# Head 0's queries straight from the projection, and in attentions 3 and 4 the division and half of the maximum's placing on GpSimd

## The reference

```python
def cross(x, ctx, mask, g):              # one layer; LN is a layer norm
    q = heads(LN(x) @ wq + bq); k = heads(ctx @ wk + bk); v = heads(ctx @ wv + bv)
    p = softmax(q @ k.T / sqrt(16) + masked)   # attentions 1, 2: an int mask; 3, 4: none
    if layer == 1: p = p * g                   # attention 1: weights 256 x 4096 after the softmax
    return x + merge(p @ v) @ wo + bo
x = cross_1(x); x += taylor_attention(LN(x)); x += top1_experts(LN(x))
x = cross_2(x); x += frame_attention(LN(x)); x += chosen_experts(LN(x))
x = cross_3(x); x += plain_attention(LN(x)); x += zone_experts(LN(x))
x = cross_4(x); x += recurrence(LN(x));      x += feed_forward(LN(x))
```

## Time and profile before

| | us |
|---|---|
| median of 3 runs | 1430.35 (1428.22 to 1432.22) |
| profiled execution | 1436.41 |
| its span, first to last instruction | 1435.2 |
| busy: TensorE, VectorE, ScalarE, GpSimd | 1263.0, 1016.8, 849.1, 481.5 |
| mean granted TensorE clock | 0.935 of full speed |

### The profile page before, as it was taken

The page is one execution under the profiler, slowest core; times in us unless marked ns, Lnnn a source line. Parts: engine busy times, 40 slices in busy tenths (PEclk is TensorE's granted clock), DMA queues, the critical chain, the costliest instruction groups (busy, mean ns, idle before and its releaser), DMA issues. The chain is left out here.

```text
span 1435.2 us, 29641 instructions
## 1 busy us (share of the span) xinstructions
PE 1263.0 (88%) x10855; PEld 637.1 (44%) x10930; DVE 1016.8 (71%) x2349; ACT 849.1 (59%) x1331; POOL 481.5 (34%) x678
## 2 busy tenths in 40 slices
PE   7899978999998786899999888599998895999987
PEld 6456642333332454233333544244444581444445
DVE  4758789999997245788885243599993336999932
ACT  4632239999997230588888351178886202788852
POOL 1431317889989303344444230211110001111100
PEclk9999987999999878699999999789999996999999
DMA  8699960111140111021132426122243201122300
GB/s 293 193 323 300 331 212 19 45 50 38 39 141 2 45 30 50 19 56 48 46 94 81 151 46 234 50 57 56 68 150 109 74 0 43 56 68 63 116 1 8
DMA packets 115174, 136.61 MB, mean 95 GB/s; under 512 B 13579, under 2 KB 96179, under 8 KB 112956
## 3 DMA queue, kind: packets, MB, share of 16 engines
q1 hardware_dynamic: 107142, 126.55, 28.7%
q10 hardware_dynamic: 7888, 8.16, 1.8%
HBM read 99.73 MB, written 34.90 MB: 94 GB/s over the span
## 5 line engine op out<-in xcount | busy, mean ns | idle before, releaser
L1280 ACT ACTIVATE prob_a<-ps 128x1024 f32<-128x1024 f32 x480 | 468.4, 1019 | 96.8 <-PE ps L1103 57.8
L1085 PE MATMUL ps<-kop,qop 52*128 52x512 f16 x1024 | 302.4, 418 | 58.5 <-DMA qop<-qparts 20.9
L1304 DVE TENSOR_REDUCE best_a<-ps 128x1 f32<-128x512 f32 (+1 forms) x488 | 318.0, 710 | 24.8 <-PE ps L1085 22.8
L1103 PE MATMUL ps<-qop,kop 52*128 52x256 f16 x2048 | 217.1, 279 | 6.2 <-ACT prob_a L1280 2.7
L1132 PE MATMUL ps<-prob_a,vop_a 128*32 128x256 f32 x3072 | 212.8, 398 | 4.7 <-issue 4.7
L1300 DVE CUSTOM_DVE_ANT_0 dump_a<-ps,neg_q 128x512 bf16<-128x512 f32 (+1 forms) x244 | 165.8, 715 | 42.7 <-PE ps L1085 41.5
L1085 PEld LDWEIGHTS ps<-kop,qop 52*128 52x128 f16 x1024 | 73.1, 95 | 241.2 <-DVE best_a L1304 96.7
L1418 POOL TENSOR_TENSOR used_a<-prob_a,gT 128x1024 f32<-128x1024 f32 x64 | 154.0, 2407 | 22.2 <-DVE used_a L1317 19.4
L1396 POOL TENSOR_SCALAR mrest_a<-nmax_a 128x2 f32<-128x2 f32 x64 | 27.8, 434 | 333.1 <-DVE nmax_a L1309 333.1
L1103 PEld LDWEIGHTS ps<-qop,kop 52*128 52x128 f16 x2048 | 92.0, 96 | 105.0 <-issue 52.5
L1132 PEld LDWEIGHTS ps<-prob_a,vop_a 128*32 128x32 f32 x3072 | 86.8, 112 | 89.8 <-issue 57.0
(11 more groups left out here) (382 smaller groups left out, 1752.1 us busy)
## 6 DMA issues: line engine op xcount, KB each, us to landing
kop<-kparts SPq DMA_DIRECT2D x384, 64.0 KB, 2.3
vals<-vst SPq DMA_DIRECT2D x16, 1024.0 KB, 5.7
kparts<-kp SPq DMA_DIRECT2D x64, 256.0 KB, 4.9
vraw<-vals SPq DMA_DIRECT2D x64, 256.0 KB, 3.1
e_w<-in_e_w SPq DMA_DIRECT2D x4, 2048.0 KB, 11.3
z_w<-in_z_w SPq DMA_DIRECT2D x24, 256.0 KB, 6.4
gT<-in_ctxT SPq DMA_DIRECT2D x8, 512.0 KB, 13.3
raw<-in_mask SPq DMA_DIRECT2D x16, 256.0 KB, 3.7
```

Of the source, the lines that this page charges most:

```text
L1085: return pe.matmul(out, qop[rows, h, t * P:(t + 1) * P], kop[rows, h % UNROLL, first:first + CHUNK], start=True, stop=True)
L1103: ins = pe.matmul(st_bank(n)[:, j * NT:(j + 1) * NT], kop[rows, h % UNROLL, at:at + P], qop[rows, h, :], start=(j % 2 == 0), stop=(not add ...
L1280: act.activation(prob[:, n % NP, :], st_bank(n), ACT.Exp, scale=1.0 / SCORE_UNIT).then_inc(S("exp_done"), 1)
L1304: dve.tensor_reduce(out, bank, AX.X, ALU.max).then_inc(sem, 1)
```

## The change

Two parts. In attentions 2 to 4, head 0's queries no longer pass through DRAM: a weight matrix `first_w`, made by GpSimd during the attention before, holds head 0's columns at all their places in `qop`; two matmuls (`project_first`) make high, low and cleared rows at once, and VectorE writes them into `qop` (`set_first`). The loads begin at head 1, and TensorE waits for them and for the cleared rows only at head 1. Constants for this are made by GpSimd in stage 1 (`fill_first`: 15 instructions) from one more small load (`first_b`).

In attentions 3 and 4, ScalarE places the turned maximum in one half, and GpSimd copies it to the other (`copy_max`). The fold's result goes to bank 7 instead of a ring bank, ScalarE reads it out (`read_fold`), and GpSimd divides (`divide`: a power of −1 and a product), for all heads but the last. The order within a head is another, and the C's are 26 ahead instead of 24.

```diff
-PLAIN_ORDER = "CCKKCCV CKCKCCV KCKCF CCTCKKCV CCV".replace(" ", "")
+PLAIN_ORDER = "CCKKCV CKCCKCV CKCCFTKCCKCV CKCCV".replace(" ", "")
...
+    def project_first(self, pe, S, bank):
+        for ct in range(CT):
+            ins = pe.matmul(self.c.ps[:, bank, 0:NT], self.c.first_w[:, ct, :], self.c.xT[:, ct, :],
+                            start=(ct == 0), stop=(ct == CT - 1))
+        ins.then_inc(S("first_q_psum"), 1)
+    def set_first(self, dve, S, bank, high, whole=None, sighted=None):
+        c, l = self.c, self.l
+        found, bias = c.ps[:, bank, 0:NT], c.first_b[:, l:l + 1]
+        dve.wait_ge(S("first_q_psum"), 1)
+        if whole is None:
+            dve.tensor_scalar(high, found, c.low_row[:, 0:1], c.first_b_low[:, l:l + 1], ALU.mult, ALU.add).then_inc(S("first_q_high"), 1)
+            dve.wait_ge(S("first_q_high"), 1)
+            dve.scalar_tensor_tensor(out=c.qop[:, 0, :], in0=found, scalar=bias, in1=high, op0=ALU.add, op1=ALU.subtract)\
+               .then_inc(S("first_q_set"), 1)
+        else:
+            dve.scalar_tensor_tensor(out=whole, in0=found, scalar=bias, in1=sighted, op0=ALU.add, op1=ALU.mult)\
+               .then_inc(S("first_q_whole"), 1)
+            dve.wait_ge(S("first_q_whole"), 1)
+            dve.tensor_scalar(high, whole, c.low_row[:, 0:1], None, ALU.mult).then_inc(S("first_q_high"), 1)
+            dve.wait_ge(S("first_q_high"), 1)
+            dve.tensor_tensor(c.qop[:, 0, :], whole, high, ALU.subtract).then_inc(S("first_q_set"), 1)
...
-        self.c.ops.load_q(eng, self.c.ops.S("q_first"), slice(0, UNROLL), Q_PIECES[half::2])
+        self.c.ops.load_q(eng, self.c.ops.S("q_first"), slice(0 if self.l == 0 else 1, UNROLL), Q_PIECES[half::2])
...
+            sp.dma_start(c.first_b[:, :], c.a["first_b"]).then_inc(S("first_b_loaded"), 16)
...
+            fill_first(c, pool, S)
...
-    banks = (1, 2)
+    banks, first_bank = (2, 7), 4
...
+            q.set_first(dve, S, first_bank, first_high[:, :], first_whole[:, :], sighted[:, :])
             q.clear_blind(dve, S, banks, whole, sighted)
             q.low_of(dve, S, whole)
         else:
+            q.set_first(dve, S, first_bank, first_high[:, :])
...
+        q.project_first(pe, S, first_bank)
+        if l == SHIELDED:
+            pe.wait_ge(S("blind_found"), 1)
         q.project(pe, S, banks)
...
-            sp.dma_start(c.qop[at:at + rows, :, :], c.clear_rows[0:rows, :, :]).then_inc(S("rows_cleared"), 16)
+            sp.dma_start(c.qop[at:at + rows, 1:H, :], c.clear_rows[0:rows, 1:H, :]).then_inc(S("rows_cleared"), 16)
...
-    AHEAD = 32 if weighted else 24
+    AHEAD = 32 if weighted else 24 if by_query else 26
...
-    SUM_AT, TURN_AT = (1, 1) if weighted else (3, 4) if by_query else (3, 5)
+    SUM_AT, TURN_AT = (1, 1) if weighted else (3, 4) if by_query else (3, 4)
...
+    HALVES_SET = HALVES if by_query else 1
+    aside = lambda h: not by_query and h < H - 1
...
+    fold_out = c.ps[:, 7, 0:QT * 32]
...
-            pe.wait_ge(ops.S("q_first" if h < UNROLL else "q_rest"), Q_DONE * (l + 1))
+            if h == 0 and asked is not None:
+                pe.wait_ge(asked.S("first_q_set"), 1)
+            else:
+                pe.wait_ge(ops.S("q_first" if h < UNROLL else "q_rest"), Q_DONE * (l + 1))
...
-                pe.wait_ge(S("max_set"), HALVES * (h + 1))
+                pe.wait_ge(S("max_set"), HALVES_SET * (h + 1))
+                if HALVES_SET < HALVES:
+                    pe.wait_ge(S("max_copied"), h + 1)
...
-                        pe.wait_ge(S("max_set"), HALVES * (h + 2))
+                        pe.wait_ge(S("max_set"), HALVES_SET * (h + 2))
                     if h > 0:
                         pe.wait_ge(S("sums_read"), h)
+                    if h > 0 and aside(h - 1):
+                        pe.wait_ge(S("fold_read"), h)
...
-            bank = ring_bank()
+            bank = fold_out if aside(h) else ring_bank()
...
-            ins.then_inc(S("s_psum"), 1)
-
-        if asked is not None:
-            pe.wait_ge(asked.S("rows_cleared"), 16 * HALVES)
-        if l == KEYED:
-            pe.wait_ge(asked.S("mask_placed"), 16 * HALVES)
+            ins.then_inc(S("folded" if aside(h) else "s_psum"), 1)
...
+            if 2 * n == SC and asked is not None:
+                pe.wait_ge(asked.S("rows_cleared"), 16 * HALVES)
+            if 2 * n == SC and l == KEYED:
+                pe.wait_ge(asked.S("mask_placed"), 16 * HALVES)
...
-            for half in range(HALVES):
+            for half in range(HALVES_SET):
...
+        def read_fold(h):
+            act.wait_ge(S("folded"), h + 1)
+            if h > 1:
+                act.wait_ge(S("divided"), h - 1)
+            act.activation(folded_sums[:, h % 2, :, :], fold_out.rearrange("p (t e) -> p t e", t=QT), ACT.Copy)\
+               .then_inc(S("fold_read"), 1)
...
+                if g == TURN_AT and h > 0 and aside(h - 1):
+                    read_fold(h - 1)
...
-                elif step == "F" and h > 0:
+                elif step == "F" and h > 0 and not aside(h - 1):
...
+        def copy_max(h):
+            pool.wait_ge(S("max_set"), h + 1)
+            pool.wait_ge(S("v_filled"), h + 1)
+            if h == 1:
+                pool.wait_ge(S("bias_added"), 1)
+            if h > 2:
+                pool.wait_ge(S("divided"), h - 2)
+            pool.tensor_copy(qop[HROWS + R_MAX:HROWS + R_MASK, h, :], qop[R_MAX:R_MASK, h, :]).then_inc(S("max_copied"), 1)
+            pool.wait_ge(S("max_copied"), h + 1)
+        def divide(h):
+            pool.wait_ge(S("fold_read"), h + 1)
+            pool.tensor_tensor(rden[:, h % 2, :], folded_sums[:, h % 2, :, HD], minus_one[:, :], ALU.pow).then_inc(S("inverted"), 1)
+            pool.wait_ge(S("inverted"), h + 1)
+            pool.tensor_tensor(c.att[:, :, HD * h:HD * (h + 1)], folded_sums[:, h % 2, :, 0:HD],
+                               rden[:, h % 2, :].unsqueeze(2).to_broadcast((P, QT, HD)), ALU.mult).then_inc(S("divided"), 1)
...
+        if HALVES_SET < HALVES:
+            copy_max(0)
...
+            for ct in range(CT):
+                for half in range(HALVES):
+                    for at in (0, HD, R_LOW):
+                        first = half * HROWS + at
+                        pool.tensor_copy(c.first_w[:, ct, first:first + HD], c.wq[:, ct, 0:D:H]).then_inc(S("first_w_set"), 1)
+            pool.wait_ge(S("first_w_set"), 3 * HALVES * CT)
...
+            if h + 1 < H and HALVES_SET < HALVES:
+                copy_max(h + 1)
+            if h > 0 and aside(h - 1):
+                divide(h - 1)
```

More of the change, by code:

```diff
@@ L889, in _, with fill_first @@
                         .then_inc(S("sighted"), 1)
+def fill_first(c, pool, S):
+    step = Chain(pool, S("first_step"))
+    for i, (at, end) in enumerate(((HD, 2 * HD - 1), (HROWS + HD, HROWS + 2 * HD - 1))):
+        column = c.low_row[:, i:i + 1]
+        step(pool.memset(column, 1.0))
+        step(pool.affine_select(out=column, in_=column, compare_op=ALU.is_ge, fill=0.0, base=-at, pattern=[[0, 1]], channel_multiplier=1))
+        step(pool.affine_select(out=column, in_=column, compare_op=ALU.is_ge, fill=0.0, base=end, pattern=[[0, 1]], channel_multiplier=-1))
+    step(pool.tensor_tensor(c.low_row[:, 0:1], c.low_row[:, 0:1], c.low_row[:, 1:2], ALU.add))
+    step(pool.memset(c.mask_row[:, :], 0.0))
+    for half in range(HALVES):
+        step(pool.affine_select(out=c.mask_row[:, :], in_=c.mask_row[:, :], compare_op=ALU.not_equal, fill=MASK_UNIT,
+                                base=-(half * HROWS + R_MASK), pattern=[[0, 1]], channel_multiplier=1))
+    step(pool.memset(c.first_w[:, :, :], 0.0))
+    pool.wait_ge(S("first_b_loaded"), 16)
+    pool.wait_ge(S("q_scale"), 1)
+    step(pool.tensor_tensor(c.first_b[:, :], c.first_b[:, :], c.q_scale[:, :], ALU.mult))
+    step(pool.tensor_scalar(c.first_b_low[:, :], c.first_b[:, :], c.low_row[:, 0:1], None, ALU.mult))
+    step(pool.tensor_tensor(c.first_b[:, KEYED:KEYED + 1], c.first_b[:, KEYED:KEYED + 1], c.mask_row[:, :], ALU.add))
 def fill_constants(c, pool, S):
@@ L1211, in _ @@
         stage.reads = slots.n
+        stage.divided = 0 if by_query else H - 1
     @stage.scalar
@@ L1266, in _ @@
                     at += 1
-                if step == "F" and h > 0:
+                if step == "F" and h > 0 and not aside(h - 1):
                     slots.next()
@@ L1328, in normalise @@
                 dve.wait_ge(S("den_added"), h + 1)
+            if not by_query:
+                dve.wait_ge(S("divided"), H - 1)
             dve.reciprocal(rden[:, h % 2, :], den[:, h % 2, :] if weighted else folded[:, :, HD]).then_inc(S("den_inverted"), 1)
-            dve.wait_ge(S("den_inverted"), h + 1)
+            dve.wait_ge(S("den_inverted"), h + 1 if by_query else 1)
             dve.tensor_tensor(c.att[:, :, HD * h:HD * (h + 1)], folded[:, :, 0:HD],
@@ L1455, in _ @@
         pool.wait_ge(S("cleared"), 3)
+        if not by_query:
```

(14 more changed lines are left out.)

6 lines of the change are left out of this document (5 added, 1 removed).

## The result

| | before | after | ratio (95% interval) |
|---|---|---|---|
| first runs, median | 1429.28 (4 runs) | 1393.21 (4 runs) | 0.9749 (0.9714 to 0.9784) |
| again, five rounds | 1431.29 (9 runs) | 1394.71 (5 runs) | 0.9734 (0.9717 to 0.9752) |

A forecast was written before the change was run, and what follows sets the result against it. VectorE was taken to bound the loops of attentions 3 and 4, a transfer wait the starts. Starts 13.0 − 0.4, loops 2 × 4.0, tails 2 × 1.5 make 23.6 us off the median 1430.35: 1407, range 1397 to 1422.

The forecast's parts named there:

- C's: 512-wide score blocks on TensorE (line 1085), each costing VectorE 0.60 us.
- the head of 10.49 us: Loop of attentions 3 and 4: a VectorE floor of 9.90 plus 0.59 of waits, against 10.82 before.
- the stepping of the new order: One head of attentions 3 and 4 stepped through with TensorE's prices; the old order gave 10.79 against 10.82 measured.
- four waits: In the new head: 0.09 after the last value product, 0.29 after the double key-side groups, 0.13 at the turn, 0.08 after third value product.
- V's: Steps of two groups of the value product on TensorE (line 1132), priced 1.00 us and 0.32 to get into.
- the start of the loop: Attentions 3 and 4: a wait of 0.6 us for ring banks and 1.4 lost to the low clock.
- The starts: Starts of attentions 2 to 4: first maximum sooner by 3.0, 5.0 and 5.0 us, together 13.0.
- The tails: Attentions 3 and 4, last row maximum to last product: 1.5 us saved each, between −1 and 3.
- The clock does not stay up: Rival for the starts: the clock no longer falls, 4.5 us less in three attentions, 1402; chance 0.13.
- TensorE does not set the head at 10.8: Rival for attentions 3 and 4: the head stays at 10.8, only starts and tails gain, 1416; chance 0.14.
- The starts gained: Rival: starts gain nothing because cleared rows, mask row or heads 1 to 3 land late, 1420; chance 0.07.
- the third V does not wait: Slower rival: the head's third value-product step waits for ScalarE's fold read, 0.1 per 0.1 us beyond 0.22; 1435 at 1.22; chance 0.06.

The follow-up runs named there:

- order_alone: New kernel with the division back on VectorE and both placements back on ScalarE, no copy; of the loop's changes only order, 26 ahead and turn's place stay: head 10.35 us.
- scalar_places_both: New kernel, but ScalarE places the maximum in both halves and GpSimd copies nothing: head 10.35 us.
- six_powers: New kernel with GpSimd's power done six times instead of once: head 10.10 us.
- other_segments: New kernel with one 512-wide score block moved from the long third piece of the order to the first: head 10.36 us.
- starts_only: New kernel with the old order, division on VectorE and both placements on ScalarE; only the new starts stay: 1411.83 against 1426.68, ratio 0.9891.
- old_order: New kernel with the old order, 24 ahead and the old place of the turn; division and copy stay on GpSimd: head 10.62 us.
- the fills alone: New kernel with filling matmuls on TensorE before the first projection and behind the pairs in attentions 2 to 4: 1394.20 us.

## Why the prediction missed

**The step that failed: the head of 10.49 us, in the stepping of the new order.** It has 10.10. Two thirds of the 0.39 lie in its four waits, 0.59 us together: the runs show 0.17 for 0.29 behind the double K, 0.04 for 0.13 at the turn, none for 0.09 at the first C behind the last V, and 0.04 behind each of two other V's for 0.08 in one; with some hundredths for starting up again behind each wait, 0.33. A quarter, 0.10, is the row maximum, 0.20 for 0.30: a wait for TensorE had been booked as VectorE's own work. That the stepping gave 10.79 for the measured 10.82 proved little, since the one error filled the place of a wait that it should have found: with 0.20 and the same waits it gives 10.69 for the old order, 0.13 too little, and 10.39 for the new, 0.29 too much. Which of the stepping's prices makes its waits wrong is not shown. So the forecast gave the whole gain of the head to the division and none to the order; `order_alone` has 10.35 where that view has 10.8, and `scalar_places_both` against it shows that the division taken alone is worth nothing under the new order. The 0.39 us in 14.4 heads are 5.6 us per attention; 1.4 to 2.1 of them go back at the start of the loop, where 3.4 to 4.1 us are lost (164.09 and 163.42, less 14.8 for the pairs and 14.375 x 10.10) and not 2.0. That loss goes with the length of the low clock: in `six_powers`, 20.5 us of it instead of 23.9, it is 2.5 in attention 3 and 2.6 in attention 4.

**What the order does** is measured as waits that are gone; why they are gone is argued, not shown, from the pieces between two V's: the old one ends in CCV, where TensorE has 1.32 + 0.11 us for VectorE's 1.20, and has two C's between turn and third V where the new one has three. That such a piece makes a wait is shown for one, the 0.17 that `other_segments` removed.

**The starts** were right in attentions 3 and 4 (9.4 of 10.0). In attention 2 the first maximum came at 6.40 us for a forecast of 8.7: one subtraction, not both, met GpSimd's two-input row. 5.3 lies inside the stated 2.0 to 5.6.

**The tails** gained 3.3 and 1.7 us for a forecast of 1.5 each, and for another reason than the prediction's; that the sign was right is luck. Undisturbed, the old order takes as long: in `starts_only` attention 3's tail takes 20.03, attention 4's 16.70 us, the new kernel's 16.72. The difference is the clock. Before, attention 3:

```profile
1091.00:1094.30 3.30, 3.30 (x34) 1.71 (x28) 0.00 (x0) 1.60 (x2) 0.00 (x0) 0.50 0.00 0
...
1101.00:1104.50 3.50, 3.50 (x37) 1.79 (x40) 0.00 (x0) 1.39 (x2) 0.00 (x0) 0.52 0.02 5
```

`starts_only`, attention 4:

```profile
1360.00:1371.00 11.00, 9.05 (x128) 4.45 (x119) 0.72 (x4) 7.42 (x10) 0.00 (x0) 1.00 0.01 1
```

Two falls while TensorE runs little but V's make 20.0 us, one 18.3, none 16.7. The 5.35 us for 64 V matmuls thus held a fall of the clock, which the prediction took for V's price; without one they take 3.66 (`starts_only`, attention 4). Whether the new order prevents falls is open: two in three of the four tails with the whole old loop, at most one in those of the new loop, none in `old_order`.

**The rivals.** The clock does not stay up, against the rule on which this rival drew: without the wait for the transfer it is at 0.50 from 899.2 to 923.1. The prediction's reason against that rival (TensorE has two blocks for each 1.13 us of VectorE and idles in any case) is borne out: the fills alone moved the fall. By the Trainium skill (TensorE: Matmul & The Clock Gate, A second HAM failure mode: psum-queue depth-cycling) frequent short idle times between groups of matmuls make the clock swing between its two levels; the trace agrees on the fall, which came after gaps of 1.63 and then 0.74 us at each pair, with no transfer waited for. TensorE does not set the head at 10.8, though it does set one piece of it. The starts gained, and the third V does not wait.
